# Input gates of a GRU from split fp16 products: parts made on POOL, and the sampling matrices moved into W_ih's place

## The reference, cut to what matters

```python
def cell(h, x):
    gi = x @ W_ih + b_ih          # input gates: all 512 steps can be made ahead
    gh = h @ W_hh + b_hh          # recurrent gates: one step at a time
    i_r, i_z, i_n = jnp.split(gi, 3, axis=-1)
    h_r, h_z, h_n = jnp.split(gh, 3, axis=-1)
    r = jax.nn.sigmoid(i_r + h_r)
    z = jax.nn.sigmoid(i_z + h_z)
    n = jnp.tanh(i_n + r * h_n)
    return (1.0 - z) * n + z * h
```

## Time and profile before

| | |
|---|---|
| device time, median of 3 runs | 2293.07 us (2292.05 to 2295.16) |
| span of the profiled execution | 2285.3 us |
| recurrence, from about 769 us of the span on | 512 steps |
| busy share of PE, DVE, ACT, POOL | 95%, 68%, 56%, 22% |

### The profile page before, as it was taken

The page is one execution under the profiler, slowest core; times in us unless marked ns, Lnnn a source line. Parts: engine busy times, 40 slices in busy tenths (PEclk is TensorE's granted clock), DMA queues, the critical chain, the costliest instruction groups (busy, mean ns, idle before and its releaser), DMA issues.

```text
span 2285.3 us, 132454 instructions
## 1 busy us (share of the span) xinstructions
PE 2175.4 (95%) x56333; PEld 1835.1 (80%) x56333; DVE 1556.9 (68%) x7118; ACT 1275.1 (56%) x5574; POOL 502.0 (22%) x2261
## 2 busy tenths in 40 slices
PE   5768999999989999999999999999999999999998
PEld 3654655645545899999899999999999999999997
DVE  8986867768678366666676666666666667666665
ACT  6765947749468355566444544445454454544444
POOL 2002121021110222233222222222222222222222
PEclk8568999999999999999999999999999999999999
DMA  5000000010010000000000000000000000000000
GB/s 205 3 2 1 1 1 1 1 56 1 1 56 1 22 5 5 5 5 5 5 5 10 5 9 5 10 10 5 10 9 5 10 5 10 10 5 14 12 10 16
DMA packets 8728, 31.63 MB, mean 14 GB/s; under 512 B 1028, under 2 KB 1352, under 8 KB 7880
## 3 DMA queue, kind: packets, MB, share of 16 engines
q1 hardware_dynamic: 7712, 23.07, 2.7%
q10 hardware_dynamic: 424, 0.07, 0.0%
HBM read 18.94 MB, written 4.19 MB: 10 GB/s over the span
## 4 chain that ended last, share of the span: by engine, by line
PE 82%; DVE 11%; ACT 3%; issue 2%; DMA 1%; POOL 0%; SPq 0%; DVEq 0%; POOLq 0%; ACTq 0%
PE psum L1929 53%; PE psum L1836 9%; PE psum L1739 4%; PE psum L1660 3%; PE psum L1757 3%; PE psum L1702 3%; PE psum L1723 2%; PE psum L1863 2%; DVE region_cols L1097 2%; DVE region_cols L1081 2%; DVE top L1274 1%; PE psum L1679 1%; DMA region_cols<-in_L_cond_W_emb_dram 1%; PE psum L1772 1%; PE psum L1876 1%
## 5 line engine op out<-in xcount | busy, mean ns | idle before, releaser
L1929 PE MATMUL psum<-parts0A,region_w_hh 128*128 128x40 f16 x12288 | 430.8, 182 | 3.5 <-DVE parts0A L1503 2.5
L1929 PE MATMUL psum<-parts1A,region_w_hh 128*128 128x40 f16 x12288 | 427.4, 181 | 2.7 <-DVE parts1A L1503 2.6
L1929 PE MATMUL psum<-parts0B,region_w_hh 128*128 128x40 f16 x12288 | 427.7, 181 | 0.6 <-issue 0.5
L1929 PE MATMUL psum<-parts1B,region_w_hh 128*128 128x40 f16 x12288 | 426.6, 181 | 0.1
L1929 PEld LDWEIGHTS psum<-parts0A,region_w_hh 128*128 128x128 f16 x12288 | 382.2, 96 | 40.6 <-DVE parts0A L1503 5.8
L1929 PEld LDWEIGHTS psum<-parts1A,region_w_hh 128*128 128x128 f16 x12288 | 378.3, 96 | 40.4 <-DVE parts1A L1503 6.9
L910 ACT ACTIVATE mixA<-rzA 128x8 f32<-128x8 f32 x512 | 111.3, 217 | 535.6 <-DVE rzA L1458 535.6
L1929 PEld LDWEIGHTS psum<-parts0B,region_w_hh 128*128 128x128 f16 x12288 | 362.9, 96 | 2.0 <-issue 0.8
L1929 PEld LDWEIGHTS psum<-parts1B,region_w_hh 128*128 128x128 f16 x12288 | 361.5, 96 | 1.7 <-issue 0.2
L553 POOL TENSOR_SCALAR lineA<-lineA 128x8 f32<-128x8 f32 x511 | 121.7, 238 | 845.2 <-DVE lineA L1494 845.2
L1458 DVE TENSOR_REDUCE rzA<-psum 128x8 f32<-128x32 f32 x512 | 98.1, 192 | 249.5 <-PE psum L1929 248.1
(11 more groups left out here) (245 smaller groups left out, 3708.5 us busy)
## 6 DMA issues: line engine op xcount, KB each, us to landing
region_rows<-in_x_dram SPq DMA_DIRECT2D x4, 1024.0 KB, 11.1
region_w_a<-in_L_cond_W_qkv_dram SPq DMA_DIRECT2D x1, 3072.0 KB, 22.8
region_w_hh<-in_L_cond_W_hh_dram SPq DMA_DIRECT2D x4, 768.0 KB, 6.4
region_w_a<-in_L_cond_W_ih_dram SPq DMA_DIRECT2D x1, 3072.0 KB, 10.3
out_dram<-region_w_b SPq DMA_DIRECT2D x12, 256.0 KB, 2.2
region_cond<-in_cond_dram SPq DMA_DIRECT2D x2, 1024.0 KB, 7.6
region_cols<-in_L_cond_W_emb_dram SPq DMA_DIRECT2D x1, 2048.0 KB, 19.6
region_w_out<-in_L_cond_W_out_dram SPq DMA_DIRECT2D x1, 1024.0 KB, 21.5
```

Source lines behind the costliest of these rows:

```text
L1929: made = e.matmul(k.slots(bank)[:, :, ch, :, 0:2], k.w16[:, 2 * read + c, part, NC * "rzn".index(g) + 2 * half + ch], k.parts[now][read][: ...
```

## The change

**What it does.** The gate products of chunks 3 to 8 (rows from 128 on) take W_ih and x as two fp16 parts each, high and low, after a scaling by a power of two. One fp32 product becomes four fp16 products of the same 256 columns, added in PSUM; chunks 0 to 2 stay as they are. To make the parts:

- DVE, steps 0 to 13: two maxima of absolute values per step at the step's end (`dve_most`), 12 over 512 columns of W_ih, then 16 over 384 columns of `xT`.
- DVE, steps 16 to 21: eight tiny operations for the scales (`dve_input_scale`). POOL, step 16: one reduction over the partitions (`pool_input_most`), between its two copies of A and its two of B.
- POOL, steps 24 to 47: one piece of W_ih (128 x 256) a step, three dependent operations between its copies of A and of B: scale, copy to fp16, subtract.
- POOL, the same three for pieces of x: steps 48 to 51 for chunk 3, and 4 steps each from 68, 132, 196, 260 and 324 on for chunks 4 to 8. Pieces of W_ih and x are 48 in all.
- ACT's copy of the gates (L824) takes its scale from a tile from chunk 3 on.

The parts of W_ih lie in `rows` (24 of 32 KiB), those of x in the rest; the sampling matrices move to W_ih's place and to that of `w_out`. `dve_cuts` counts the new DVE instructions.

```diff
+FIRST_HALVED = 3
+SCALE_STEPS = {st: i for i, st in enumerate(range(16, 22))}
+PART_STEPS = {24 + i: i for i in range(W_PIECES)}
...
-        self.sampling = view("rows", 0, FP32, B, NC, D)
+        self.sampling = [view("w_a", 8 * b, FP32, NC, D) for b in range(B - 1)] + [view("w_out", 0, FP32, NC, D)]
...
+        self.w_parts = view("rows", 0, FP16, 2, NC, GATES * D)
+        self.x_parts = [view("rows", 24 + 4 * i, FP16, 2, NC, B, LONG) for i in range(2)]
...
             pool_state(e, k, st, half)
+            if st in SCALE_STEPS and SCALE_STEPS[st] == half == 0:
+                pool_input_most(e, k)
+            if half == 0 and st in PART_STEPS:
+                pool_weight_part(e, k, PART_STEPS[st])
+            if half == 0 and st in HALVED_STEPS:
+                pool_input_part(e, k, *HALVED_STEPS[st])
...
+def pool_input_most(e, k):
+    s = k.sem
+    e.wait_ge(s["in_scale"], 2)
+    e.partition_all_reduce(k.in_most[:], k.in_power[:], P, bass.bass_isa.ReduceOp.max).then_inc(s["ih_most"], 1)
...
+    e.tensor_scalar(k.scaled, k.w_ih[:, c, cols], k.in_scale[:, 0:1], None, ALU.mult).then_inc(s["w_scaled"], 1)
+    e.wait_ge(s["w_scaled"], i + 1)
+    e.tensor_copy(k.w_parts[:, 0, c, cols], k.scaled).then_inc(s["w_halved"], 1)
+    e.wait_ge(s["w_halved"], i + 1)
+    e.tensor_tensor(k.w_parts[:, 1, c, cols], k.scaled, k.w_parts[:, 0, c, cols], ALU.subtract).then_inc(s["w_lowered"], 1)
...
+    e.tensor_reduce(k.ih_most[:, i:i + 1], given, AX.X, ALU.max, apply_absolute_value=True).then_inc(s["ih_most"], 1)
...
+        if st < MOST_STEPS:
+            dve_most(e, k, 2 * st)
+            dve_most(e, k, 2 * st + 1)
...
-        made = e.matmul(k.bank(SIDE_BANK[number % 2], B * LENGTHS[q]), k.w_ih[:, c, block * P:(block + 1) * P],
-                        k.xT[:, c, :, STARTS[q]:STARTS[q] + LENGTHS[q]], start=(c == 0), stop=(c == NC - 1))
+        for part in range(2):
+            for low in range(2):
+                made = e.matmul(to, k.w_parts[:, part, c, cols], k.x_parts[q % 2][:, low, c],
+                                start=(c == part == low == 0), stop=(c == NC - 1 and part == low == 1))
```

More of the change, by code:

```diff
@@ L146, in side_done, with halved_steps @@
     return [(group, number % 2) for group, number, part in SIDE.get(s, ()) if part[-1] == NC - 1]
+FIRST_HALVED = 3
+MOST_PIECES = GATES * NC + NC * B
+HALVED_FROM = STARTS[FIRST_HALVED]
+MOST_STEPS = MOST_PIECES // 2
+SCALE_STEPS = {st: i for i, st in enumerate(range(16, 22))}
+SCALE_OPS = (2, 1, 1, 2, 1, 1)
+W_PIECES = 2 * GATES * NC
+PART_STEPS = {24 + i: i for i in range(W_PIECES)}
+def halved_steps():
+    table = {}
+    for q in range(FIRST_HALVED, CHUNKS):
+        at = 24 + W_PIECES if q == FIRST_HALVED else STARTS[q - 2] + 4
+        for c in range(NC):
+            table[at + c] = (q, c)
+    return table
+HALVED_STEPS = halved_steps()
 FREE = [st for st in range(2 * LONG) if st >= LONG and not side_done(st)]
@@ L368, in layout @@
         self.both = small("both", GATES, NC)
+        self.ih_most = small("ih_most", MOST_PIECES)
+        self.scaled = view("w_b", 20, FP32, HALF_ROW)
+        self.in_most = small("in_most", 2)
+        self.in_power = small("in_power", 2)
+        self.in_scale = small("in_scale", 2)
+        self.in_unscale = small("in_unscale", 1)
+        self.w_parts = view("rows", 0, FP16, 2, NC, GATES * D)
+        self.x_parts = [view("rows", 24 + 4 * i, FP16, 2, NC, B, LONG) for i in range(2)]
     def slots(self, i):
@@ L543, in pool_hat @@
     b, c = divmod(n, NC)
-    mine = k.sampling[:, b, c, c * P:(c + 1) * P]
+    mine = k.sampling[b][:, c, c * P:(c + 1) * P]
     e.wait_ge(s["hat"], 2 * n + 2)
@@ L823, in act_take_gates @@
             e.wait_ge(s[f"put{h}"], STARTS[q - 1])
-    e.activation(k.gates_in[q][:, j], k.bank(bank, B, LENGTHS[q]), ACT.Identity, scale=scale,
+    if q == FIRST_HALVED and j == 0:
+        e.wait_ge(s["in_scale"], 8)
+    e.activation(k.gates_in[q][:, j], k.bank(bank, B, LENGTHS[q]), ACT.Identity, scale=scale if q < FIRST_HALVED else k.in_unscale[:],
                  bias=k.bias_in[:, m, g, ch:ch + 1]).then_inc(s["gates_in"], 1)
@@ L860, in act_hat @@
         e.wait_ge(s["hat"], 2 * n + 1)
-        e.activation(k.sampling[:, b, c], k.away[:, n % 2], ACT.Relu, scale=-1.0, bias=k.ones[:, 0:1]).then_inc(s["hat"], 1)
+        e.activation(k.sampling[b][:, c], k.away[:, n % 2], ACT.Relu, scale=-1.0, bias=k.ones[:, 0:1]).then_inc(s["hat"], 1)
     else:
@@ L1528, in pe_program @@
                 made = e.matmul(k.bank(part, HALF_ROW)[32 * b:32 * b + 32], k.xT[:, c, b, rows],
[L1529 removed]
+                                k.sampling[b][:, c, part * HALF_ROW:(part + 1) * HALF_ROW],
                                 start=(c == 0), stop=(c == NC - 1), tile_position=(0, 32 * b))
@@ L1834, in pe_gate_products @@
             e.wait_ge(s["plus_w_out"], NC * B)
-    for c in products:
-        made = e.matmul(k.bank(SIDE_BANK[number % 2], B * LENGTHS[q]), k.w_ih[:, c, block * P:(block + 1) * P],
-                        k.xT[:, c, :, STARTS[q]:STARTS[q] + LENGTHS[q]], start=(c == 0), stop=(c == NC - 1))
+    to = k.bank(SIDE_BANK[number % 2], B * LENGTHS[q])
+    cols = slice(block * P, (block + 1) * P)
+    if q >= FIRST_HALVED and products[0] == 0:
+        e.wait_ge(s["x_lowered"], NC * (q - FIRST_HALVED + 1))
+        if q == FIRST_HALVED:
+            e.wait_ge(s["w_lowered"], W_PIECES)
+    for c in products:
+        if q < FIRST_HALVED:
+            made = e.matmul(to, k.w_ih[:, c, cols], k.xT[:, c, :, STARTS[q]:STARTS[q] + LENGTHS[q]], start=(c == 0), stop=(c == NC - 1))
+            continue
+        for part in range(2):
+            for low in range(2):
+                made = e.matmul(to, k.w_parts[:, part, c, cols], k.x_parts[q % 2][:, low, c],
+                                start=(c == part == low == 0), stop=(c == NC - 1 and part == low == 1))
     if products[-1] == NC - 1:
@@ L1862, in pe_row_products @@
     for c in products:
-        made = e.matmul(k.bank(SIDE_BANK[number % 2], HALF_ROW), k.xT[:, c, b, tile * P:(tile + 1) * P], k.sampling[:, b, c, cols],
+        made = e.matmul(k.bank(SIDE_BANK[number % 2], HALF_ROW), k.xT[:, c, b, tile * P:(tile + 1) * P], k.sampling[b][:, c, cols],
                         start=(c == 0), stop=(c == NC - 1))
@@ L1876, in pe_late_products @@
         made = e.matmul(k.bank(SIDE_BANK[number % 2], HALF_ROW), k.xT[:, c, b, LATE[1] - P:LATE[1]],
-                        k.sampling[:, b, c, part * HALF_ROW:(part + 1) * HALF_ROW], start=(c == 0), stop=(c == NC - 1))
+                        k.sampling[b][:, c, part * HALF_ROW:(part + 1) * HALF_ROW], start=(c == 0), stop=(c == NC - 1))
     if products[-1] == NC - 1:
```

70 lines of the change are left out of this document (67 added, 3 removed).

## The result

| | before | after |
|---|---|---|
| device time, median | 2292.56 us (4 runs, 2288.79 to 2295.16) | 2313.04 us (4 runs, 2307.08 to 2321.61) |
| span of the profiled execution | 2285.3 us | 2319.7 us |
| recurrence, first low A to the 511th | 1503.4 us | 1537.2 us |

The account below looks back on a forecast made before the run. A step was taken as the longer of PE's sum and the 2.887 us loop from low B. -11.5 + 3.1 + 10.4 + 1.5 + 13.3 = +16.8 us gave 2309.9 us, range 2290 to 2332.

Parts of the forecast that it names:

- The gain, -11.5: Gate steps of chunks 3 to 8: cheaper fp16 products save 0.040 us in each of 288 steps, -11.5 us.
- PE's sum, or the loop of 2.887: Every recurrence step lasts the longer of PE's summed work and the loop from low B over PE, DVE, ACT back.
- the change doesn't do what it says: Rival at the gate products: four fp16 products take 0.51 us, so no 11.5 gain; 2321 us, chance 0.05.
- The maxima, +3.1: DVE, steps 0 to 13: maxima delay the next r sum, steps 3.53 or 3.27 us long, +3.1 us.
- The reduction, +10.4 and +1.5: POOL, step 16: reconfiguring there and back stalls the next step, +10.4 us; PE's lower clock afterwards adds +1.5.
- the way back is free: Rival at POOL's reduction: returning to scalings and copies costs nothing, the 7.30 had another cause; 2301.1 us, chance 0.15.
- The parts, +13.3: POOL, 48 part steps: its operations block DVE, lengthening the loop by 0.30 to 3.19 us, +13.3 us.
- runs behind it: Part steps: DVE's high B, due at 0.63, waits for POOL's scaling to end at 0.86 and ends at 0.93.
- Heavier blocking: Rival in the 48 part steps: early subtraction or slow scaling costs 0.6 to 1.05 us each; 2324 to 2346, chance 0.17.
- The 7.8 us between span and median: Whole kernel: median 2293.07 lies 7.8 us above the profiled span of 2285.3, taken as unchanged by the change.

Follow-up runs that it names:

- the last two runs: Changed kernel with the parts' three operations behind POOL's copies of B, 2332.87 us; changed kernel with the subtraction one step later, ahead of the next scaling, 2329.52 us.
- the two cheap versions: Changed kernel with constant scales, W_ih's parts in steps 0 to 23, no product of low parts: three narrow matmuls 2300.54 us, two wide ones 2298.15 us.
- the preparation alone: Changed kernel with its maxima, reduction and parts, but the parts go to a tile nobody reads and gate products stay fp32: 2313.62 us, ratio 1.009.

## Why the prediction was right, and where it was not

The sign, the range and nearly the size came true, but partly by luck, as two errors cancelled: the gain of 11.5 was nearly all eaten by stalls that the forecast did not have (some +10), and the parts were priced 6.7 too high. The maxima and the reduction were off by less than 1 us together.

**The gain, -11.5: the step that failed.** Its working held where it was tested alone: the products take 0.44, the loop is 2.887, undisturbed gate steps last that. The claim behind it, "PE's sum, or the loop of 2.887", left out a third bound, the supply of instructions, at which the kernel before already stood. Over the 384 steps the floor fell from 1123.3 to 1115.3, as forecast (11.5 less, 3.5 for the parts of x), and the measured length rose from 1127.3 to 1140.8. The stalls took 25.5 us where before had 4.0 and 8.7. The rival "the change doesn't do what it says" had the right outcome, no gain, for the wrong reason.

**The maxima, +3.1.** Steps 0 to 5 last 3.505, the next eight 3.238, against 3.53 and 3.27: +2.7. Right.

**The reduction, +10.4 and +1.5.** 5.83 there, 0.37, 7.21 back, as read from the earlier trace rows; the two steps behind it took 13.93 and 4.17 us, 12.25 more than two of 2.927. Right, the lower clock included; "the way back is free" falls. The rows show PE at the lower clock for some 5 us, and the second of the two steps lost 1.2 us.

**The parts, +13.3: mis-sized.** The 28 steps with an fp32 product were 3.02 to 3.06 long, +3.1 together, not +7.3; the 20 with fp16 products +3.5, not +6.0. So 6.6, half. The step that failed is that high B "runs behind it", the scaling: it ran beside it, 0.13 longer. The earlier trace rows showed a long copy that blocks, and I carried this over to every POOL operation; the last two runs show that it depends on POOL's operation. Two more errors lay inside: the scaling takes 0.93, outside the 0.40 to 0.75 that I allowed, and POOL was left with 0.15 us idle in the step. Heavier blocking (2324 to 2346) was real all the same, but at another order of the operations: 3.33 us when the subtraction meets low A or, in the two cheap versions, low B, and 3.44 when it meets high B.

The Trainium skill's rule (SBUF — State Buffer, Who interferes with whom), that the later of the two waits for the whole of the earlier, agrees with the subtraction's rows (0.59 and 0.54 us) and not with the scaling's (0.34 beside an operation of 0.93).

**The sum.** With the sizes from the traces: -11.5 + 2.7 + 12.3 + 6.6 = +10. The profiled executions, a short one of before and the longest of after, lie 34 us apart, the difference being stalls of PE (21.5 us more in the 384 steps, some more behind them); the median lost 20.5, so that in a usual execution the stalls took some 10 more than before, nearly the whole gain. That agrees with the preparation alone costing the same as the whole. It is worked out, not read from a trace: only the longest of the four executions has one. The 7.8 us between span and median, which the forecast carried over, are no fixed cost: 1.8 us of them are, and the rest is that the profiled execution of before was a short one. The forecast doesn't suffer, since it comes to the median plus 16.8.

**What stays open.** Why a block takes 3.8 us, and why the same count stalls in one chunk and hardly in another. In the trace of after the starts of these transfers mostly lie 3.3 to 4.4 us apart and a transfer takes 1.1; the next one starts 1.1 us behind the end of a hole, as if only one were under way at a time, but no run tested that. The Trainium skill (Runtime: NRT & Kernel Launch, Instruction fetch mechanics) says that each engine's stream is refilled in blocks of 16 KiB, 256 instructions, the next while the current one runs, and calls the cost "mostly hidden". The rows agree with the block; what it hides ends at some 67 instructions a us on PE here.

## What to carry to other kernels

Before pricing a cheaper matmul, count instructions: PE's loads and matmuls of a step over its length, against the blocks of 256 in the instruction queue (here one every 3.8 us on average, at best). In this kernel, which stood at that rate, splitting one product into more but cheaper ones gained nothing, nor did leaving the products out at the same count; fewer instructions did. An operation that changes POOL's configuration belongs where nobody waits for POOL for 13 us, and POOL's subtraction of two inputs must not meet a DVE operation of the critical loop, however short that one is. Work on POOL is nearly free in steps whose length PE sets, as W_ih's parts were in steps 0 to 15.

## What the runs showed of the hardware that was not expected

- PE's instructions come in blocks of 256, one every 3.79 to 3.85 us on average when PE takes them as fast as it can: 66.5 to 67.5 instructions a us over 384 steps. The stalls that were counted in the trace of after are 0.2 to 0.55 us each, and the profile calls them "issue".
- Below that rate the times of 8 runs spread over 2.1 us. Kernels at or beyond it spread over 3.7 to 14.5 us (4 to 17 runs each), the change most of all.
- A scaling of 256 columns on POOL takes 0.93 us with its factor from a tile and 0.86 with a constant, against 0.40 for a cast and 0.67 for a two-input subtraction; high B beside it takes 0.34 and 0.26.
- POOL's return from the reduction costs 7.2 to 7.3 us even for a minus of 8 columns, more than the 5.6 to 5.8 of the way there.
